# A graph attention layer with one head: the four row sums, the old sum and the clearing of rows change places

## The chip, the cores and the metric

The kernel runs on one core of a Trainium2 chip. The metric is the device time of one launch in microseconds (us); the times below are of the kernel before the change. The engines are TensorE (PE; its weight loads are listed as PEld), VectorE (DVE), ScalarE (ACT), GpSimd (POOL) and SyncE (SP, which here only issues DMAs).

## The reference, cut to what matters

A graph has 1250 nodes and 20,000 edges, with rows of 768 floats. Two attention layers run one after the other (8 heads, then 1 head), and a relational layer and a graph convolution follow.

```python
def gatv2(x, src, dst, Ws, bs, Wd, bd, attn):
    fs = (x @ Ws + bs).reshape(-1, H, D)
    fd = (x @ Wd + bd).reshape(-1, H, D)
    e = leaky_relu(fs[src] + fd[dst], 0.2)
    logits = einsum('ehd,hd->eh', e, attn)
    m = segment_max(logits, dst, num_segments=N)
    ex = exp(logits - m[dst])
    denom = segment_sum(ex, dst, num_segments=N)
    alpha = ex / denom[dst]
    out = segment_sum(alpha[:, :, None] * fs[src], dst, num_segments=N)
    return elu(out)
h = gatv2(x, ..., W1s, ..., attn1)        # 8 heads of 96
h = layer_norm(h + x, ln1_w, ln1_b)
out = gatv2(h, ..., Wos, ..., attno)      # 1 head of 768: the "second attention"
return layer_norm(out, lno_w, lno_b)
```

## The kernel before

**Tiles and groups.** The nodes are sorted by degree and laid out in 10 tiles of 128. A *group* is 128 nodes of one tile with S = 4 incoming edges each. There are 48 groups in this input, run as 12 turns of a loop with U = 4 groups in its body (index `u`). The softmax is kept running: each group brings four rows, its logits raise the maximum `top`, the sum so far in `acc` is scaled down by a factor, and the group's weighted rows are added.

**The stages.** Each stage ends at a barrier of all engines: sorting of edges, projection of x, the first attention (`attention("first", HEADS, ...)`), `settle(True)`, which normalises and projects for the second attention, the second attention (`attention("second", 1, ...)`), `settle(False)`, the 34 relations, two gather stages and the output. The change touches the second attention and `settle(True)`.

**A group in the second attention.** The order on each engine is the order of its code; semaphores join them.

- POOL (`gather_edges`) gathers the edge record (L799) and, two groups ahead, the four rows `row` of 128 x 776 (L804, four DMAs). Between them it makes the masks `val` and `neg` (L826 to L829). A row buffer is free again when PE has counted `summed` for the group that used it.
- The sum fs + fd: DVE adds `fdt` to rows 0 and 1 (L1049). PE adds it to rows 2 and 3 in PSUM (`pS`), as a product of the identity with the row and one with `fdt` (L994, L996).
- DVE takes the leaky part times the attention vector with its sum for all four rows (L1072), in PSUM for two of them. This gives the logits.
- DVE `arguments` (L1090 to L1100) makes the exponents. ACT takes the exponential (L970) and scales the old sum, `scaled` = `acc` times the factor (L977).
- DVE `weigh` (L1106 to L1121) makes four diagonal matrices `shares` from the weights (L1110, four instructions). PE multiplies them with the four rows into `pA` (L1014). DVE `finish` (L1079) adds `pA` and `scaled` into `acc`.

**The order within a turn.** DVE does, for each u: `arguments(u)`, `add(u + 1)` (the sums and logits of the next group), `finish(u - 1)`, `weigh(u)`. PE does `add(u + 2)` and then the four products of group u. Each product of PE with f32 operands of 128 x 384 appears in the trace as two passes, and a row has two halves, so a row's product is four passes.

**The clearing.** The relational stage writes only some of the rows of `y_d`; the others are set to zero before it. SP does this with a loop of DMAs from a zeroed tile `nothing` (L932), each waited for before the next one is issued. It runs in the second attention's SP block, beside the groups.

Of the kernel before, what the change touches and what calls it, by code (L numbers as in the profile page):

```python
# [11 lines left out]
P = 128  # L12
# [55 lines left out]
def gnn_kernel(nc, io, out):  # L68
    ctx = ExitStack()
    with ctx:  # L70
# [800 lines left out]
        def attention(name, heads, attn, fd_table):  # L871
# [5 lines left out]
            with stage() as st:  # L877
# [19 lines left out]
                pS = [pb(f"pS{j}", [P, 2, 512], F32, st) for j in range(S // 2)]  # L897
                nothing = sb("nothing", [P, D], F32, st)
                att_in, dve_step, init_ok, fd_in, zeroed, y_zero, sp_posted = sems(
                    st, "att_in", "dve_step", "init_ok", "fd_in", "zeroed", "y_zero", "sp_posted")  # L900
                sum_ok = Signal(st, "sum_ok", S // 2, U, U)
# [17 lines left out]
                with nc.Block() as block:  # L919
                    @block.sync  # L920
                    def _(sp):
                        sp.dma_start(attr[:], attn.rearrange("h d -> (h d)").partition_broadcast(P)).then_inc(att_in, 16)
                        sp.wait_ge(att_in, 16)
                        if fd_table is None:

                            sp.wait_ge(zeroed, 1)

                            tiles = tiles_of(sp)
                            behind = sp.value_load(ctl[0:1, C_BEHIND:C_BEHIND + 1], min_val=1, max_val=RT)
                            with sp.Fori(0, behind) as n:  # L930
                                sp.wait_ge(y_zero, n * 16)
                                sp.dma_start(y_d[ds(((tiles + n) * P).with_bounds(min_val=0, max_val=RT * P), P), :],  # L932
                                             nothing[:]).then_inc(y_zero, 16)
                            sp.wait_ge(y_zero, behind * 16)
                            sp.sem_inc(sp_posted, 1)

# [82 lines left out]
                    def _(dve):  # L1019
# [4 lines left out]
                        v = Steps(dve, dve_step)  # L1024
                        dve.memset(nothing[:], 0.0).then_inc(zeroed, 1)
                        v.mark(dve.memset(acc[:], 0.0))
# [110 lines left out]
                        finish(turns, -1, last)  # L1137

        attention("first", HEADS, io["L0_gnn_attn1"], fd_d[0:N])

        rcnt = sb("rcnt", [P, NT + 1, RELS], F32)

        def settle(first):
# [11 lines left out]
            with stage() as st:  # L1155
# [25 lines left out]
                placed = sems(st, "placed0", "placed1")  # L1181
                f_out = sems(st, "f_out0", "f_out1")
                low_ok = Signal(st, "low_ok", 1, 2, 2)
                exp_ok = Signal(st, "exp_ok", 1, 2, 2)
# [31 lines left out]
                with nc.Block() as block:  # L1216
                    @block.sync
                    def _(sp):
# [8 lines left out]
                        sp.wait_ge(v_in, 16 * (NW + 3))  # L1227
                        sp.wait_ge(w_in, 16 * NW)

                    @block.gpsimd  # L1230
# [115 lines left out]
                    def _(dve):  # L1346
# [6 lines left out]
                        pre.link(dve.reciprocal(rden[:], rden[:]))  # L1353
                        if first:
                            for b in range(2):
                                pre.link(dve.memset(of[b][:, D:W], 0.0))
                        else:
                            pre.link(dve.tensor_reduce(csum[:], cntge[:].rearrange("p t (s r) -> p t r s", s=S), X, ALU.add))
                            pre.link(dve.tensor_copy(csum[:, :, 0], degr[:]))
                            pre.link(dve.tensor_tensor(rcnt[:], csum[:, :, 0:RELS], csum[:, :, 1:RELS + 1], ALU.subtract))  # L1360
                            pre.link(dve.tensor_scalar(rcnt[:], rcnt[:], 1.0, None, ALU.max))
                            pre.link(dve.reciprocal(rcnt[:], rcnt[:]))
# [83 lines left out]

        settle(True)
        attention("second", 1, io["L0_gnn_attno"], None)
        settle(False)


# [423 lines left out]
```

## Time and profile before

| | |
|---|---|
| median of 3 runs | 4282.16 us (4281.59 to 4284.36) |
| the profiled execution's own time | 4274.83 us |
| its span | 4273.1 us |
| `settle(True)` | about 1132 to 1336 us of the span |
| second attention | about 1337 to 1885 us of the span |
| `settle(False)` | from about 1886 us |

The rows that the prediction uses come from this execution. *Granted clock* is the TensorE clock that the chip allowed, 1.00 for 2.4 GHz and 0.5 for 1.2 GHz. "Idle before" an instruction is put down to whatever released it last. "x2" in a timeline row is two passes merged, with the time from the start of the first to the end of the last.

### The profile page before, as it was taken

What the parts mean: (1) busy time and instruction counts of PE and PEld (TensorE: products, weight loads), DVE (VectorE), ACT (ScalarE), POOL (GpSimd) and SP (SyncE); (2) the same over time, 40 slices, a digit from 0 to 9 for tenths busy, and PEclk for the clock granted to TensorE, in tenths of its full rate; (3) what the DMA queues carried; (4) which work ended last, traced back from release to release, by engine and by line L of the source; (5) the groups of instructions that cost most, each with busy time, mean ns of one, the idle gap of its engine ahead of it and who ended that gap; (6) DMA issues with size and microseconds to landing.
All of it is one profiled execution on the core that took longest, in us unless ns stands there. A gap on an engine that the chain in (4) does not pass through costs nothing. (4 is left out here: it accounts for less than half of the span.)

```text
span 4273.1 us, 61931 instructions
## 1 busy us (share of the span) xinstructions
PE 2822.8 (66%) x12224; PEld 2123.7 (50%) x12225; DVE 2608.4 (61%) x5744; ACT 1177.6 (28%) x4467; POOL 2034.2 (48%) x2781
## 2 busy tenths in 40 slices
PE   0295877778697999967799999999997000080000
PEld 0153444444354555533599999999997000040000
DVE  8234888888666788866555555555553666515555
ACT  0011655566421111113344444444443000010000
POOL 0474766667456777731111111111112777517776
PEclk6697988998898999988899999999999555595555
DMA  0233433333314765541355556555554666506665
GB/s 23 87 90 116 120 105 105 105 105 106 133 41 136 249 202 151 152 133 45 113 184 181 185 175 185 183 180 182 177 182 141 183 187 183 181 37 203 196 203 176
DMA packets 198954, 621.95 MB, mean 146 GB/s; under 512 B 42375, under 2 KB 87259, under 8 KB 198683
## 3 DMA queue, kind: packets, MB, share of 16 engines
q0 software_dynamic: 95696, 414.22, 32.6%
q1 hardware_dynamic: 53628, 139.21, 10.6%
q10 hardware_dynamic: 49536, 67.66, 4.4%
q14 instruction: 83, 0.68, 0.0%
q8 instruction: 11, 0.18, 0.0%
HBM read 503.34 MB, written 117.91 MB: 145 GB/s over the span
## 5 line engine op out<-in xcount | busy, mean ns | idle before, releaser
L1603 PE MATMUL pO<-wh,gT 128*128 128x384 f32 x4128 | 1093.0, 338 | 0.5 <-DVE wl L1641 0.5
L1603 PEld LDWEIGHTS pO<-wh,gT 128*128 128x128 f32 x4128 | 749.8, 188 | 0.8 <-DVE wl L1641 0.8
L1603 PE MATMUL pO<-wl,gT 128*128 128x384 f32 x2064 | 691.1, 335 | 0.0
L804 POOL DMA_INDIRECT row<-fs_d,rec x400 | 441.1, 1103 | 163.0 <-issue 122.0
L994 PE MATMUL pS<-row,ident 128*128 128x384 f32 x800 | 361.6, 536 | 237.7 <-DVE sj L1069 149.5
L1627 DVE TENSOR_SCALAR cntge<-pT 128x768 int32<-128x768 int32 x173 | 165.6, 957 | 566.7 <-PE pT L501 563.7
L508 PE MATMUL pO<-wt,hT 128*128 128x384 f32 (+1 forms) x1200 | 420.1, 512 | 41.4 <-ACT hT L1314 19.6
L1556 ACT ACTIVATE gT<-cntge 128x256 fp32r<-128x256 f32 x1038 | 371.7, 411 | 165.0 <-PE pO L1603 122.9
L501 PE MATMUL pT<-ident,ht 128*128 128x128 f32 (+1 forms) x240 | 39.6, 310 | 558.0 <-ACT ht L1764 440.7
L960 ACT ACTIVATE sj<-sj 128x96 f32<-128x96 f32 x1176 | 313.0, 268 | 281.7 <-DVE sj L1069 281.7
L1603 PEld LDWEIGHTS pO<-wl,gT 128*128 128x128 f32 x2064 | 388.7, 188 | 0.0
L994 PEld LDWEIGHTS pS<-row,ident 128*128 128x128 f32 x800 | 159.3, 208 | 381.2 <-DVE sj L1069 183.9
L996 PE MATMUL pS<-fdt,ident 128*128 (+1 forms) x800 | 346.8, 517 | 0.0
L1538 POOL COPY gindex<-source 128x1 int32 x172 | 49.8, 289 | 621.3 <-DMA g<-hr_d,gindex 621.3
L508 PEld LDWEIGHTS pO<-wt,hT 128*128 128x128 f32 (+1 forms) x1200 | 236.7, 200 | 214.9 <-issue 68.5
L1527 POOL DMA_INDIRECT g<-hr_d,gindex x173 | 168.9, 976 | 355.4 <-PE pT L501 350.2
L501 PEld LDWEIGHTS pT<-ident,ht 128*128 128x128 f32 (+1 forms) x240 | 32.3, 159 | 574.2 <-ACT ht L1764 441.0
L1566 ACT ACTIVATE nrow<-pO 128x384 f32<-128x384 f32 x344 | 166.0, 483 | 537.2 <-PE pO L1603 537.2
L1719 DVE SCALAR_TENSOR_TENSOR acc<-row,val,acc 128x768 f32 x192 | 196.5, 1024 | 155.8 <-DMA row<-xs_d,rec 150.7
L799 POOL DMA_INDIRECT rec<-by_dst_d,index x204 | 219.3, 1075 | 85.3 <-issue 78.9
L804 POOL DMA_INDIRECT row<-xs_d,rec x200 | 226.3, 1131 | 61.9 <-issue 61.6
L1014 PE MATMUL pA<-row,shares 128*128 128x384 f32 x768 | 255.5, 486 | 0.0
(287 smaller groups left out, 5019.7 us busy)
## 6 DMA issues: line engine op xcount, KB each, us to landing
raw<-in_L_gnn_W_rel_dram SPq DMA_DIRECT2D x204, 384.0 KB
y_d<-nrow ACTq DMA_DIRECT2D x344, 192.0 KB
y_d<-nothing SPq DMA_DIRECT2D x53, 384.0 KB, 2.7
row<-fs_d,rec POOLq DMA_INDIRECT x400, 4.6
fs_d<-of SPq DMA_DIRECT2D x9, 388.0 KB
fd_d<-of SPq DMA_DIRECT2D x9, 388.0 KB, 2.6
xt<-in_x_dram SPq DMA_DIRECT2D x9, 384.0 KB, 4.2
h_d<-ht SPq DMA_DIRECT2D x9, 384.0 KB, 4.1
```

Of the source, the lines that this page charges most:

```text
L508: last = pe.matmul(dst[0:rows, q, 0:HALF], rows_t[:, c * P:c * P + rows], w[:, c, lo:up], start=c == 0, stop=c == KC - 1)
L799: pool.indirect_dma_start(b["rec"][u][:], None, table_rows, bass.IndirectOffsetOnAxis(ap=b["index"][u][:], axis=0)).then_inc(b["rec_in"][u ...
L804: pool.indirect_dma_start(b["row"][u][:, j, :], None, table, bass.IndirectOffsetOnAxis(ap=b["rec"][u][:, 2 * j + field:2 * j + field + 1], ...
L960: last = act.activation(of_head, of_head, ACT.Copy, accum_out=dots[off % U][:, j, h:h + 1])
L994: pe.matmul(pS[j][:, q, 0:HALF], ident[:], row[off % U][:, S // 2 + j, lo:up], start=True, stop=False)
L996: last = pe.matmul(pS[j][:, q, 0:HALF], ident[:], fdt_row(tile)[:, lo:up], start=False, stop=True)
L1014: last = pe.matmul(pA[:, q, 0:HALF], share, row[u][:, j, lo:up], start=j == 0, stop=j == S - 1)
L1527: pool.indirect_dma_start(g[:], None, hr_d, bass.IndirectOffsetOnAxis(ap=gindex[:], axis=0))\
L1556: act.activation(gT[:, c].bitcast(F32R), cut[:, :, c * P:(c + 1) * P], ACT.Copy).then_inc(gT_ok.sem, 1)
L1566: act.activation(y[:, lo:up], pO[:, q, 0:HALF], ACT.Copy).then_inc(evac_ok.sem, 1)
L1603: last = pe.matmul(pO[:, q, 0:HALF], gT[:, c, half, :].bitcast(F32R), w[:, c, lo:up].bitcast(F32R), start=c == 0 and k == 0, stop=c == KC ...
L1719: dve.scalar_tensor_tensor(out=into, in0=b["row"][u][:, j, :], scalar=w[:, j:j + 1], in1=into, op0=ALU.mult, op1=ALU.add).then_inc(used.se ...
```

## The change

A function `attention_single` takes the place of `attention` for one head.

- PE adds `fdt` to row 3 alone; DVE adds it to rows 0, 1 and 2. `pS` has two buffers, one for each of two groups.
- The diagonal matrices become one tile `share` of five, made by one instruction of 128 x 640. The fifth (index 0) holds the factor of the old sum. PE multiplies it with `acc` as a last product into `pA`. `pA` has two buffers.
- ACT no longer scales the old sum; it moves the finished `pA` into `acc`.
- `finish` on DVE is gone.
- The order on PE is now: the products of group u, then the old sum's product, then `add(u + 2)`. The order on DVE is `arguments(u)`, `dot(u + 1)`, `weigh(u)`.
- The clearing of `y_d` and its zeroed tile move into the SP and DVE blocks of `settle(True)`. There SP reaches it after its waits for the stage's weights.

The diff, cut to its core (the memset and the SP loop are removed from `attention` word for word as they stand in `settle` below):

```diff
+        def attention_single():
+            BY_PE = S - 1
...
+                    @block.scalar
+                    def _(act):
...
+                        def keep(i, off, tile):
+                            total.wait(act, i, off)
+                            act.activation(split(of(acc, tile)), halves(pA[off % 2]), ACT.Copy).then_inc(kept.sem, 1)
...
+                            for u in range(U):
+                                ex_in.wait(act, i, u)
+                                shared.wait(act, i, u - 2)
+                                act.activation(pe_[u % 2][:], ex[u % 2][:], ACT.Exp).then_inc(ex_ok.sem, 1)
+                                keep(i, u - 1, t[u])
...
+                        def add(i, off, tile):
+                            rows_wait(pe, b, i, off)
+                            logits.wait(pe, i, off - 2)
+                            for q, lo, up in HB:
+                                pe.matmul(pS[off % 2][:, q, 0:HALF], ident[:], row[off % U][:, BY_PE, lo:up],
+                                          start=True, stop=False)
+                                last = pe.matmul(pS[off % 2][:, q, 0:HALF], ident[:], of(fdt, tile)[:, lo:up],
+                                                 start=False, stop=True)
+                            last.then_inc(sum_pe.sem, 1)
...
+                            for u in range(U):
+                                shared.wait(pe, i, u)
+                                kept.wait(pe, i, u - 2)
+                                for j in range(S):
+                                    for q, lo, up in HB:
+                                        last = pe.matmul(pA[u % 2][:, q, 0:HALF], share[u % 2][:, 1 + j, :], row[u][:, j, lo:up],
+                                                         start=j == 0, stop=False)
+                                last.then_inc(summed.sem, 1)
+                                kept.wait(pe, i, u - 1)
+                                for q, lo, up in HB:
+                                    last = pe.matmul(pA[u % 2][:, q, 0:HALF], share[u % 2][:, 0, :], of(acc, t[u])[:, lo:up],
+                                                     start=False, stop=True)
+                                last.then_inc(total.sem, 1)
+                                add(i, u + 2, t[u + 2])
...
+                        def dot(i, off, tile):
+                            rows_wait(dve, b, i, off)
...
+                            for j in range(BY_PE):
+                                logits.wait(dve, i, off - 1, j + 1)
+                                dve.tensor_tensor(leak[:, j, :], row[off % U][:, j, 0:D], fd[:, 0:D], ALU.add)\
+                                   .then_inc(sum_ok.sem, 1)
...
+                            for j in range(S):
+                                if j < BY_PE:
+                                    sum_ok.wait(dve, i, off, j + 1)
+                                    ins = dict(out=leak[:, j, :], in0=leak[:, j, :], in1=attr[:])
+                                else:
+                                    logits.wait(dve, i, off - 1, j + 1)
+                                    sum_pe.wait(dve, i, off)
+                                    ins = dict(out=split(leak[:, j, :]), in0=halves(pS[off % 2]), in1=split(attr[:]))
...
+                        def weigh(v, i, u, tile):
+                            k = u % 2
+                            ex_ok.wait(dve, i, u)
+                            v.link(dve.tensor_tensor(pe_[k][:, 1:S + 1, 0], pe_[k][:, 1:S + 1, 0], val[u][:], ALU.mult))
+                            total.wait(dve, i, u - 2)
+                            den_ok.wait(dve, i, u - 1)
+                            sh = [P, S + 1, P]
+                            v.mark(dve.tensor_tensor(share[k][:], over(ident[:], 1, sh), pe_[k][:].to_broadcast(sh), ALU.mult))
+                            v.mark(dve.tensor_reduce(dsum[:], pe_[k][:, 1:S + 1, 0], X, ALU.add))
...
+                            v.wait()
+                            dve.sem_inc(shared.sem, 1)
...
+                            for u in range(U):
+                                top_ok.wait(dve, i, u - 1)
+                                arguments(v, i, u, t[u])
+                                dot(i, u + 1, t[u + 1])
+                                weigh(v, i, u, t[u])
...
+                        if first:
+                            sp.wait_ge(zeroed, 1)
+                            tiles = tiles_of(sp)
+                            behind = sp.value_load(ctl[0:1, C_BEHIND:C_BEHIND + 1], min_val=1, max_val=RT)
+                            with sp.Fori(0, behind) as n:
+                                sp.wait_ge(y_zero, n * 16)
+                                sp.dma_start(y_d[ds(((tiles + n) * P).with_bounds(min_val=0, max_val=RT * P), P), :],
+                                             nothing[:]).then_inc(y_zero, 16)
+                            sp.wait_ge(y_zero, behind * 16)
+                            sp.sem_inc(sp_posted, 1)
...
-        attention("second", 1, io["L0_gnn_attno"], None)
+        attention_single()
```

On PE, in the loop of the second attention, where one group's sums meet another group's products. Before (the last sums of group 3, then the products of group 1; `row1_2` is row buffer 1 of this stage, and REGISTER_ALU and ISA are address and semaphore work):

```order
L994 MATMUL pS1_2<-row3_2,ident 128x384
L996 MATMUL pS1_2<-fdt,ident 128x384
L994 MATMUL pS1_2<-row3_2,ident 128x384
L996 MATMUL pS1_2<-fdt,ident 128x384
L555 REGISTER_ALU x2
L1014 MATMUL pA_2<-row1_2,shares 128x384 x2
L555 REGISTER_ALU
L1014 MATMUL pA_2<-row1_2,shares 128x384 x6
```

And now, at the same place:

```order
L1221 MATMUL pA1<-row1_2,share1 128x384 x8
L1226 REGISTER_ALU x2
L1226 ISA
L1226 MATMUL pA1<-acc,share1 128x384
L1226 ISA
L1226 MATMUL pA1<-acc,share1 128x384
L555 REGISTER_ALU
L1204 MATMUL pS1_2<-row3_2,ident 128x384
L1206 REGISTER_ALU x2
L1206 ISA
L1206 MATMUL pS1_2<-fdt,ident 128x384
```

The sums of group u + 2 stood ahead of the products of group u and stand behind them now; the product with `acc` has come in between.

On DVE, the end of one group's logits and what follows, in the same loop. Before:

```order
L1072 SCALAR_TENSOR_TENSOR sj,dots_2<-pS_2,attr 128x768 x2
L555 REGISTER_ALU
L1079 REGISTER_ALU
L1079 ISA
L1079 TENSOR_TENSOR acc<-pA,scaled 128x768
L1106 TENSOR_TENSOR pe_2<-pe_2,val_2 128x4
L50 REGISTER_ALU
L1110 TENSOR_SCALAR shares<-ident,pe_2 128x128 x4
L1117 TENSOR_REDUCE dsum<-pe_2 128x1
```

And now:

```order
L1266 SCALAR_TENSOR_TENSOR leak,dots_2<-leak,attr 128x768
L555 REGISTER_ALU
L1266 SCALAR_TENSOR_TENSOR leak,dots_2<-pS_2,attr 128x768
L1289 TENSOR_TENSOR pe_2<-pe_2,val_2 128x4
L50 REGISTER_ALU
L1293 TENSOR_TENSOR share<-ident,pe_2 128x640
L1294 TENSOR_REDUCE dsum<-pe_2 128x1
```

The step on `pA` is gone, one of the two steps that read `pS` is left and is the last one ahead of the weights, and four diagonal instructions have become one.

## Rows read from the trace of the kernel before

**Rows 1.** Busy time by stretch: us, PE, PEld, DVE, ACT, POOL, granted clock, DMA share, GB/s.

```profile
1217.00:1237.00 20.00, 18.94 (x64) 11.23 (x63) 13.84 (x23) 5.98 (x7) 13.78 (x14) 1.00 0.16 40
...
1375.00:1560.00 185.00, 180.81 (x554) 103.88 (x553) 147.84 (x460) 24.56 (x38) 132.51 (x188) 1.00 0.72 244
1560.00:1885.00 325.00, 319.50 (x980) 184.47 (x978) 259.45 (x804) 43.08 (x66) 221.96 (x321) 1.00 0.49 146
```

**Rows 2.** Second attention's PE passes with `shares`: durations in ns, first and last start.

```profile
L1014 PE MATMUL pA<-row,shares x768: 486/486/486, 1378.6 to 1882.9; 128*128 128x384 f32 x192
```

**Rows 3.** Groups of instructions by shape, 1560 to 1870 us: busy us, mean ns, idle before.

```profile
L1049 DVE TENSOR_TENSOR sj<-row,fdt 128x768 f32<-128x768 f32 x60 | 54.8, 954 | 10.3 <-issue 10.3
...
L977 ACT ACTIVATE scaled<-acc,pe 128x768 f32 x29 | 27.1, 936 | 223.5 <-DVE acc L1079 223.5
```

**Rows 4.** Timeline of one group of the second attention: start, us, engine, instruction.

```profile
1604.31 5.32 PE L1014 MATMUL pA<-row,shares 128*128 128x384 f32 x16
...
1607.07 0.95 DVE L1072 SCALAR_TENSOR_TENSOR sj<-pS,attr 128x768 f32<-128x768 f32 x1
...
1607.95 0.08 DVE L1072 DVE_READ_ACCUMULATOR sj<-pS,attr 128x1 f32 x1
...
1610.46 0.95 POOL L804 DMA_INDIRECT row<-fs_d,rec  x1 [0.99 <-PE pA L1014]
1610.65 0.15 DVE L1106 TENSOR_TENSOR pe<-pe,val 128x4 f32<-128x4 f32 x1
...
1610.84 0.88 DVE L1110 TENSOR_SCALAR shares<-ident,pe 128x128 f32<-128x128 f32 x4
...
1611.64 0.14 DVE L1117 TENSOR_REDUCE dsum<-pe 128x1 f32<-128x4 f32 x1
...
1611.88 0.16 DVE L1121 TENSOR_TENSOR den<-den,dsum 128x1 f32 x1
...
1621.15 0.95 POOL L804 DMA_INDIRECT row<-fs_d,rec  x1 [0.30 <-issue]
```

**Rows 5.** Timeline of the stage's first groups: where DVE waits for a sum of PE.

```profile
1358.21 0.81 PE L996 MATMUL pS<-fdt,ident 128*128 128x384 f32 x2
...
1359.06 0.96 DVE L1072 SCALAR_TENSOR_TENSOR sj<-pS,attr 128x768 f32<-128x768 f32 x1 [0.90 <-PE pS L996]
...
1371.09 0.95 DVE L1079 TENSOR_TENSOR acc<-pA,scaled 128x768 f32 x1
```

**Rows 6.** Timeline of the first attention: PE's first passes after it sat idle.

```profile
463.84 0.91 PE L994 MATMUL pS<-row,ident 128*128 128x384 f32 x2 [1.84 <-DMA row<-fs_d,rec]
...
508.65 1.65 PE L994 MATMUL pS<-row,ident 128*128 128x384 f32 x2 [2.76 <-DVE sj L1069]
...
941.65 1.65 PE L994 MATMUL pS<-row,ident 128*128 128x384 f32 x2 [2.42 <-DVE sj L1069]
...
1120.03 0.91 PE L994 MATMUL pS<-row,ident 128*128 128x384 f32 x2 [2.41 <-DVE sj L1069]
```

**Rows 7.** Busy time by stretch, columns as in Rows 1: behind two of these pauses.

```profile
508.00:515.00 7.00, 6.35 (x10) 3.52 (x11) 6.79 (x13) 7.00 (x52) 4.93 (x7) 0.51 0.26 65
...
941.00:947.00 6.00, 5.35 (x12) 3.08 (x13) 5.97 (x9) 6.00 (x47) 4.26 (x7) 0.72 0.00 0
```

**Rows 8.** The clearing by its tile: SP's issues in ns, first and last start.

```profile
L932 SPq DMA_DIRECT2D y_d<-nothing x53: 332/332/370, 1342.8 to 1543.4; - x53
...
L932 SPq DMA_DIRECT2D y_d<-nothing x2: 332/332/332, 1522.2 to 1524.6; - x2
```

**Rows 9.** DMA issues by line: KB each, us to landing.

```profile
wt<-in_L_gnn_Wod_dram SPq DMA_DIRECT2D x1, 2304.0 KB, 20.3
```

**Rows 10.** Timeline: SP's last load of `settle(True)`, DVE's last copy, the next stage's memset.

```profile
1136.46 0.69 SPq L1226 DMA_DIRECT2D wt<-in_L_gnn_Wod_dram  x1
...
1336.11 0.14 DVE L1442 COPY fdt<-lin 128x1 f32<-128x1 f32 x1
...
1338.74 0.70 DVE L1025 MEMSET nothing<- 128x768 f32 x1 [2.48 <-issue]
```

More of the change, by code:

```diff
@@ L897, in attention @@
                 pS = [pb(f"pS{j}", [P, 2, 512], F32, st) for j in range(S // 2)]
-                nothing = sb("nothing", [P, D], F32, st)
-                att_in, dve_step, init_ok, fd_in, zeroed, y_zero, sp_posted = sems(
-                    st, "att_in", "dve_step", "init_ok", "fd_in", "zeroed", "y_zero", "sp_posted")
+                att_in, dve_step, init_ok, fd_in = sems(st, "att_in", "dve_step", "init_ok", "fd_in")
                 sum_ok = Signal(st, "sum_ok", S // 2, U, U)
@@ L923, in _ @@
                         sp.wait_ge(att_in, 16)
[L924 to L935, printed above, removed]
                     @block.gpsimd
@@ L1024, in _ @@
                         v = Steps(dve, dve_step)
-                        dve.memset(nothing[:], 0.0).then_inc(zeroed, 1)
                         v.mark(dve.memset(acc[:], 0.0))
@@ L1182, in settle @@
                 f_out = sems(st, "f_out0", "f_out1")
+                if first:
+                    nothing = sb("nothing", [P, D], F32, st)
+                    zeroed, y_zero, sp_posted = sems(st, "zeroed", "y_zero", "sp_posted")
                 low_ok = Signal(st, "low_ok", 1, 2, 2)
@@ L1228, in _ @@
                         sp.wait_ge(w_in, 16 * NW)
+                        if first:
+                            sp.wait_ge(zeroed, 1)
[7 more added lines that the diff above has]
+                            sp.sem_inc(sp_posted, 1)
                     @block.gpsimd
@@ L1354, in _ @@
                         if first:
+                            dve.memset(nothing[:], 0.0).then_inc(zeroed, 1)
                             for b in range(2):
```

108 lines of the change are left out of this document (added).

## The prediction

> **What bounds the kernel now.** The views were read in this order: the busy time by stretch, the passes of one tile, the groups of instructions, and then the timeline of single groups. The first shows that in the second attention PE is busy in 319.5 of 325 us, at the full clock of 2.4 GHz, while DVE is busy in 259.5 [rows 1]. So PE's passes set the pace there. The pace: the first of the 768 passes with `shares` starts at 1378.6 and the last at 1882.9, and that last one is the 16th of its group [rows 2]. Sixteen passes last 5.32 us and a single one 0.486, so they start (5.32 - 0.486) / 15 = 0.322 apart [rows 2, 4]. A group's period is then (1882.9 - 15 x 0.322 - 1378.6) / 47 = 10.63 us. PE's own need is 32 passes (16 for two row sums, 16 for four products) x 0.322 = 10.3. PE never waits long, because the sums of group u + 2 stand ahead of the products of group u: while PE does them, DVE makes the weights that the products need. The reader should note that this order, more than the number of passes, is what keeps PE busy.
>
> **PE's passes: fewer.** One row sum is dropped (8 passes), and the old sum's product is added (4). 28 passes x 0.322 = 9.0 us of work. If nothing else changed, PE would allow 1.3 us less per group.
>
> **DVE's work: about the same.** It gains one sum of 954 ns [rows 3] and loses the step on `pA`, 0.95 [rows 5]. Four diagonal instructions, 0.88 together [rows 4], become one of 640 elements. No row has that form. It is sized between 0.15 for 4 elements and 954 ns for 768 [rows 3, 4]: (0.954 - 0.15) / 764 = 1.05 ns an element, so 0.15 + 636 x 0.00105 = 0.82 us, and the next instruction starts some 0.08 before its end, as it does behind the four: 0.74. The ends: 0.6 if it ran faster than a two-operand step, 0.9 if it ran as slowly as the four. DVE's busy time stays 259.45 / 325 x 10.63 = 8.5 us per group, and with its short waits between small steps about 9.3.
>
> **ACT.** The move of `pA` replaces the scaling, 936 ns [rows 3]. Reading PSUM may make it shorter, or at worst twice as long. ACT sits idle for 223.5 us in 29 groups, 7.7 each [rows 3], and PE asks for the moved sum only behind 16 passes of the next group, so I cost it at nothing. If that cover were gone, its 0.9 would be paid in full.
>
> **The order: this is the main term.** Now PE does the products of group u - 1, the old sum, and only then `add(u + 1)`. DVE reads that sum in the last step of `dot(u + 1)`, which stands ahead of `weigh(u)`, and PE can't start group u without the weights. So the two wait for each other in turn, and a period is the sum of four pieces:
> - DVE from the read of `pS` to the signal `shared`: 0.88 for the step (1607.07 to 1607.95), 0.19 for the weights' mask (1610.65 to 1610.84), 0.74 for `share`, 0.24 for the two small steps (1611.64 to 1611.88) [rows 4]. Sum 2.05.
> - The signal to PE. No row isolates it; PE's signal to DVE took 0.04, from 1358.21 + 0.81 to 1359.06 [rows 5]. I take 0.05; the ends are 0.02 and 0.3.
> - PE: 27 x 0.322 + 0.486 = 9.18, and 0.10 more, since two passes behind a pause take 0.91 and not 0.81 [rows 5, 6]. Sum 9.28.
> - The signal back, 0.04 [rows 5].
>
> The period is 2.05 + 0.05 + 9.28 + 0.04 = 11.42 us, against 10.63. That is 0.79 x 47 = 37 us **more**. DVE's remaining work, 9.3 - 2.05 = 7.3, and the few register loads at a turn's start fit beside PE's 9.28. The ends of the stage change little: the first group no longer waits behind a step on `pA`, which started at 1371.09 [rows 5], and the last group has the old sum, the move and a superfluous `add` behind it. I take 0, with 3 us either way.
>
> **PE's clock.** PE now pauses 11.42 - 9.28 = 2.1 us in each group. In the first attention PE also pauses, and what follows is in the rows: behind 1.84 us its first two passes take 0.91, behind 2.76 us they take 1.65; behind 2.42 us they take 1.65, and behind 2.41 us 0.91 [rows 6]. The two long ones go with a granted clock of 0.51 over 7 us and 0.72 over 6 us [rows 7], so PE was at 1.2 GHz for nearly all of the first stretch and for 0.56 of the second. The second costs 6 x 0.28 = 1.7 us, the first 7 x 0.49 = 3.4. A pause of 2.1 lies between one that cost nothing and a pair of which one cost. I take one group in four at 1.7, the nearer row: 0.43 x 47 = 20 us. The ends are 0 and one fall in each group, 80 us. All of it would lie on the path, since PE is in the chain.
>
> **The clearing.** In `settle(True)` SP can begin when the last weights have landed, 1136.46 + 20.3 = 1156.8 [rows 9, 10], and its register loads are done; these took from the end of the memset, 1339.44 [rows 10], to 1342.8 [rows 8], 3.4 us. So it begins at 1160.2. Its 53 DMAs ran one behind the other at (1543.4 - 1342.8) / 52 = 3.86 us, and at 2.4 where nothing was in the way [rows 8]. The stage's last work ends at 1336.11 + 0.14 = 1336.25 [rows 10], so there are 176 us, or 3.3 us for each. The DMA engines' share is 0.16 in `settle(True)` and 0.49 in the attention when the clearing is over [rows 1]; by that, a third of the 1.46 us between the two paces: 53 x 2.9 = 154, done by 1314. Hidden: nothing is paid, and nothing is gained in the attention, where PE was as busy with the clearing beside it (180.8 of 185) as without [rows 1]. If the old pace held, the last would land at 1160.2 + 53 x 3.86 = 1364.8, and the barrier would come 28 us late. The moved memset, 0.70 [rows 10], stands ahead of the stage's first step: +0.7.
>
> A rule speaks against this cover. The Trainium skill, "DMA: Bandwidth & Descriptors", section "Issuing engines are not separate DMA queues", says that DMAs issued by SP and by GpSimd end up on the same 16 DMA engines and interleave. By that rule moving the clearing to another stage doesn't take its competition away, and with as many transfers of GpSimd beside it as before the sum would be 28 us higher; the trace's long and short times between issues agree that it is slowed by others.
>
> **The sum.** 37 + 20 + 0.7 = 58 us. The profiled execution took 4274.8 us, 7.3 below the median of the three runs, so it would become 4332; against the median, 4282.2 + 58 = **4340 us**.
>
> **Rivals.**
> - *The clock falls in most groups.* Each fall costs 1.7 at least and so makes the period longer without making the pause shorter; nothing in the loop cures it. With a fall in most groups, 47 x (0.79 + 1.4) = 103, so 4386. For it: one of the two pauses of 2.4 fell. Against: the pause here is shorter than those. 28%.
> - *The clearing outlasts its stage*, at the old pace: 4340 + 28 = 4368. For it: SP waits for each DMA. Against: the share of 0.16. 6%.
> - *The other side: the loop isn't closed through the new order.* The decisive point is whether PE's sum for the next group is there when DVE comes to read it. If DVE found it ready, because the four pieces come to less than 10.6 together (0.8 less than my sum), then the pace would be that of POOL, whose own turn from gather to gather is 1621.15 - 1610.46 = 10.69 with its slow masks and, by the wait of 0.30 to 0.99 ahead of it, hardly under 10.3 [rows 4]. A period of 10.3 gives 47 x (-0.33) = -15, so 4267. For it: PE has 4 passes less and buffers are doubled. Against: the order of the rows on both engines has no way round. 7%.
> - *The serial loop as computed, few falls:* 4340, itself between 4310 (short `share`, no fall) and 4365. 59%.
>
> **How the numbers follow.** About 0.2% (8.6 us) is what a measurement of this kernel can tell from no change. The range reaches from 4308, the serial loop with its cheap ends, to 4400, a fall in nearly every group with the serial loop's upper ends; it leaves out the faster case, part of the clearing's sum with the clock's, and the very worst. Of the 7% on the other side I give 5 to faster and 2 to same, and 1 more to same for a serial loop with all its pieces at their low ends. Faster 0.05, same 0.03, slower 0.92.
>
> **What would show it.** In the trace of the changed kernel: the passes with `share` at a period of 11.4 to 12.5 us; the step of DVE on `pS` waiting for PE some 1.5 to 2 us in each group; PE waiting about 2.1 us for the DVE ahead of the first product with `share`; a granted clock of 0.9 to 1.0 in the stage, and under 0.9 if the second case holds; POOL waiting for PE by about 1 us per group, where it hardly did. The last `y_d` DMA should be issued by 1315, with `settle(True)` ending at 1337. The prediction is wrong if DVE doesn't wait at `pS`, if the period is under 10.6, or if SP is the last at the barrier of `settle(True)`.

## The result, and the profile after

| | before | after |
|---|---|---|
| median on the same chip (4 runs each) | 4281.88 us (4277.8 to 4284.36) | 4378.73 us (4373.06 to 4383.2) |
| ratio, 95% interval | | 1.0226 (1.0209 to 1.0244) |
| profiled execution's own time / span | 4274.83 / 4273.1 us | 4381.81 / 4380.1 us |
| second attention | 547.9 us | 643.5 us |

The change costs 97 us. The forecast was 58 us and its range 26 to 118. The stage's time runs between two rows of SP, its first DMA in the stage and its first in `settle(False)`. Timeline of before:

```profile
1337.67 0.34 SPq L922 DMA_DIRECT2D attr<-in_L_gnn_attno_dram  x1
...
1885.58 0.34 SPq L1219 DMA_DIRECT2D lnw<-in_L_gnn_lno_w_dram  x1
```

And of after:

```profile
1341.16 0.34 SPq L1165 DMA_DIRECT2D attr<-in_L_gnn_attno_dram  x1
...
1984.65 0.34 SPq L1396 DMA_DIRECT2D lnw<-in_L_gnn_lno_w_dram  x1
```

So the stage has nearly all of it: 643.5 - 547.9 = 95.6 us, with 1.2 more in `settle(True)` by the same kind of rows. (The two profiled executions are 107 us apart. The other 10 lie in stages ahead and behind whose code is the same, and the four executions of the changed kernel alone spread over 10 us.) The passes with `share` and DVE's instruction that makes it (after, by tile: durations in ns, first and last start):

```profile
L1221 PE MATMUL pA<-row,share x768: 486/486/1004, 1373.9 to 1979.4; 128*128 128x384 f32 x192
...
L1293 DVE TENSOR_TENSOR share<-ident,pe x48: 824/826/846, 1372.8 to 1973.4; 128x640 f32<-128x640 f32 x48
```

The period is (1973.4 - 1372.8) / 47 = **12.78 us**, where [rows 2] gave 10.63. Some passes last up to 1004 ns. The busy time by stretch (after, columns as in Rows 1) says the same of the whole stage: PE is busy in 83% of the time, where [rows 1] show 98%, and the granted clock is 0.90.

```profile
1400.00:1560.00 160.00, 132.53 (x354) 73.35 (x355) 111.81 (x308) 16.29 (x28) 86.08 (x142) 0.90 0.41 129
1560.00:1700.00 140.00, 115.73 (x310) 63.73 (x309) 95.42 (x265) 15.06 (x25) 72.62 (x121) 0.90 0.41 125
1700.00:1960.00 260.00, 214.98 (x572) 118.35 (x570) 174.76 (x483) 27.61 (x46) 139.81 (x224) 0.90 0.41 125
```

The loop itself is in the timeline (after; start, us, engine, instruction):

```profile
1449.96 0.96 DVE L1266 SCALAR_TENSOR_TENSOR leak<-pS,attr 128x768 f32<-128x768 f32 x1 [3.46 <-PE pS L1206]
...
1451.03 0.83 DVE L1293 TENSOR_TENSOR share<-ident,pe 128x640 f32<-128x640 f32 x1
...
1452.10 5.43 PE L1221 MATMUL pA<-row,share 128*128 128x384 f32 x16 [2.18 <-DVEq L1298]
...
1460.59 0.81 PE L1206 MATMUL pS<-fdt,ident 128*128 x2
1461.44 0.96 DVE L1266 SCALAR_TENSOR_TENSOR leak<-pS,attr 128x768 f32<-128x768 f32 x1 [1.79 <-PE pS L1206]
...
1463.59 7.12 PE L1221 MATMUL pA<-row,share 128*128 128x384 f32 x16 [2.18 <-DVEq L1298]
```

Read it down: DVE takes the sum in `pS` at 1449.96, makes `share`, and PE starts at 1452.10; PE's last sum ends at 1461.40, and DVE, which has stood for 1.79 us, takes it at 1461.44. Each engine waits for the other once in a group. One turn is 2.14 + 9.30 + 0.04 = 11.48. The next group begins behind a pause of the same 2.18 us, but its sixteen passes last 7.12 us instead of 5.43, and the group took 13.25. Not all of the sixteen are slow: by stretches of 1 us from 1464 to 1468 the granted clock was 0.59, 0.50, 0.50 and 0.70, and it was 1.00 ahead of them and behind, so about 3.4 us ran at 1.2 GHz.

Groups of instructions (after, 1400 to 1960 us; busy us, mean ns, idle before):

```profile
L1221 PE MATMUL pA<-row,share 128*128 128x384 f32 x704 | 292.9, 580 | 97.1 <-DVEq L1298 97.1
...
L1266 DVE SCALAR_TENSOR_TENSOR leak<-pS,attr 128x768 f32<-128x768 f32 x44 | 42.1, 958 | 118.4 <-PE pS L1206 118.4
...
L804 POOL DMA_INDIRECT row<-fs_d,rec x179 | 174.4, 974 | 190.5 <-PE pA L1221 147.5 <-issue 43.0
...
L1181 ACT ACTIVATE acc<-pA 128x768 f32 x44 | 35.7, 811 | 250.3 <-PE pA L1226 250.3
```

POOL now waits 147.5 / 44 = 3.4 us per group; it isn't what holds the stage up. The clearing, by its tile (after):

```profile
L1412 SPq DMA_DIRECT2D y_d<-nothing x53: 332/333/376, 1161.0 to 1303.0; - x53
```

### The profile page after: what moved, and what is told of

Same layout as the page of the kernel before. It is cut to its first block and busy times, and to the rows that moved or that the text cites. A ratio compares the mean times of both kernels' runs of the same rounds, so it can differ in the third digit from the quotient of the medians.

```text
span 4380.1 us, 61353 instructions
## 1 busy us (share of the span) xinstructions
PE 2822.5 (64%) x12016; PEld 2111.0 (48%) x12017; DVE 2610.7 (60%) x5599; ACT 1158.8 (26%) x4468; POOL 1980.6 (45%) x2781
## 5 line engine op out<-in xcount | busy, mean ns | idle before, releaser
L804 POOL DMA_INDIRECT row<-fs_d,rec x400 | 424.8, 1062 | 302.1 <-PE pA L1221 147.5
L1744 ACT ACTIVATE gT<-cntge 128x256 fp32r<-128x256 f32 x1038 | 358.0, 408 | 182.3 <-PE pO L1791 139.1
L1221 PE MATMUL pA<-row,share 128*128 128x384 f32 x768 | 320.5, 581 | 113.0 <-DVEq L1298 113.0
L980 PE MATMUL pS<-row,ident 128*128 128x384 f32 x400 | 192.5, 567 | 209.9 <-DVE sj L1054 161.5
L1221 PEld LDWEIGHTS pA<-row,share 128*128 128x128 f32 x768 | 169.6, 226 | 263.8 <-DVEq L1298 100.9
L799 POOL DMA_INDIRECT rec<-by_dst_d,index x204 | 237.6, 1164 | 86.6 <-issue 83.7
L1000 PE MATMUL pA<-row,ident 128*128 128x384 f32 x768 | 255.5, 486 | 0.0
```

The costliest lines, as they stand in the source:

```text
L799: pool.indirect_dma_start(b["rec"][u][:], None, table_rows, bass.IndirectOffsetOnAxis(ap=b["index"][u][:], axis=0)).then_inc(b["rec_in"][u ...
L804: pool.indirect_dma_start(b["row"][u][:, j, :], None, table, bass.IndirectOffsetOnAxis(ap=b["rec"][u][:, 2 * j + field:2 * j + field + 1], ...
L980: pe.matmul(pS[j][:, q, 0:HALF], ident[:], row[off % U][:, S // 2 + j, lo:up], start=True, stop=False)
L1000: last = pe.matmul(pA[:, q, 0:HALF], share, row[u][:, j, lo:up], start=j == 0, stop=j == S - 1)
L1221: last = pe.matmul(pA[u % 2][:, q, 0:HALF], share[u % 2][:, 1 + j, :], row[u][:, j, lo:up], start=j == 0, stop=False)
L1744: act.activation(gT[:, c].bitcast(F32R), cut[:, :, c * P:(c + 1) * P], ACT.Copy).then_inc(gT_ok.sem, 1)
```

## The experiments

The theory after the result: the order closes the loop (some 40 us), and the clock falls behind most of the pauses that the loop makes (some 60). The rival: one of the other parts costs the time (the product with `acc`, the third sum on DVE, the moved clearing, POOL). Each ratio below is to the kernel before on the same chip, with its 95% interval.

### The order alone, undone and done

In the changed kernel, PE's sums go back ahead of the products:

```diff
                             for u in range(U):
+                                add(i, u + 2, t[u + 2])
                                 shared.wait(pe, i, u)
...
-                                add(i, u + 2, t[u + 2])
```

> The changed kernel with one thing moved back: PE does the sums of group u + 2 ahead of the products of group u, as before the change. Theory (PE and DVE wait for each other in turn because the sums stand behind the products): the wait of DVE at pS, 1.8 to 3.5 us a group, goes, and so does PE's pause of 2.2; the period drops from 12.78 to the next bound, POOL's own turn of 10.3 to 10.7 us, so 4270 to 4290 us. Rival 1 (the new work itself is what costs: the product with the old sum, its move by ACT, one more sum on DVE): the period stays near 12.8, about 4379 us. Rival 2 (only the clock's falls cost): 11.5 a group, about 4318 us.

Measured: 4284.61 us, 1.0005 (0.9995 to 1.0015). One line takes back the whole loss. The kernel with the sums first, by tile and by stretch:

```profile
L1293 DVE TENSOR_TENSOR share<-ident,pe x48: 824/826/828, 1373.0 to 1873.6; 128x640 f32<-128x640 f32 x48
```

```profile
1560.00:1700.00 140.00, 121.23 (x367) 68.38 (x366) 112.28 (x315) 16.42 (x29) 102.75 (x144) 1.00 0.52 148
```

The period is 500.6 / 47 = 10.65, the clock full. But PE has 4 passes fewer than before and still gains nothing. Its groups (1400 to 1840 us) show that it waits for rows, and that POOL, which fetches them, waits for nobody ("issue" is POOL's own time between its instructions):

```profile
L804 POOL DMA_INDIRECT row<-fs_d,rec x166 | 214.4, 1291 | 50.9 <-issue 50.9
...
L1204 PE MATMUL pS<-row,ident 128*128 128x384 f32 x164 | 70.4, 511 | 56.8 <-DMA row<-fs_d,rec 56.8
```

The same edit the other way round, in the kernel before: PE's sums behind the products, nothing else changed.

```diff
                             for u in range(U):
-                                add(i, u + 2, t[u])
...
+                                if heads == 1:
+                                    add(i, u + 2, t[u])
```

> The kernel before the change with only PE's order in the second attention taken from the change: products of group u first, the sums of group u + 2 behind them. No other part of the change. Theory: the loop closes here too; 0.88 (last step on pS) + 0.87 (step on pA) + 0.19 + 0.28 (first diagonal matrix) + 0.05 + 10.57 (32 passes) + 0.04 = 12.9 us at full clock with a pause of 2.3, and 1.7 more where the clock falls: 4282 + 47 x (12.9 - 10.63) = 4389 us without falls, up to 4469 with one in every group, 4450 with three in four. Rival (the order alone does little as long as PE has 32 passes to keep it busy): 4282 to 4300 us.

Measured: 4425.59 us, 1.0334 (1.0317 to 1.0351). Its groups (1400 to 1840 us):

```profile
L1014 PE MATMUL pA<-row,shares 128*128 128x384 f32 x514 | 197.4, 543 | 74.4 <-DVE shares L1112 72.0 <-DVE acc L1081 2.3
...
L1074 DVE SCALAR_TENSOR_TENSOR sj<-pS,attr 128x768 f32<-128x768 f32 x65 | 62.3, 958 | 119.7 <-PE pS L996 107.0 <-issue 12.7
```

The same mutual waits, without any other part of the change. With two rows in `pS` to read and 32 passes the loop is longer, and it costs 142 us. The timeline of PE divides them: a group without a slow clock takes 12.91 us (from 1408.02 to 1420.93), as the expectation had it, which makes (12.91 - 10.63) x 47 = 107, and 21 of the 47 groups behind a pause of 2.32 us or a little more are slower, by 1.5 to 1.7 us each. The order is the cause in both kernels.

A third way to open the loop leaves PE's order as changed and moves DVE's step on `pS` behind `weigh`:

```diff
-                            for j in range(S):
+                            logits_of(i, off, range(BY_PE))
...
                                 weigh(v, i, u, t[u])
+                                logits_of(i, u + 1, [BY_PE])
```

> The changed kernel with PE's order as changed, but DVE takes the last step of the next group's logits, the one that reads pS, behind weigh instead of ahead of it. Theory (a loop through both engines): opening it on DVE's side is as good as on PE's side, period 10.3 to 10.7 us, 4270 to 4295 us, and PE is ahead of DVE at pS. Rival (it is the place of PE's sums that costs, whatever DVE's order, since rows and PSUM come free later): near 4379 us.

Measured: 4291.86 us, 1.0025 (1.0013 to 1.0036). The loop is open; the period is 10.98, and POOL again waits for nobody.

### The clock alone

Three products of PE (six passes) whose result isn't used are put into the pause, behind the sums; then one product only:

```diff
                                 add(i, u + 2, t[u + 2])
+                                for k in range(3):
+                                    pe.matmul(pA[(u + 1) % 2][:, k % 2, 0:HALF], ident[:], fdt[:, 0, 0:HALF],
+                                              start=True, stop=True)
```

> The changed kernel with three further products behind the sums of each group (six passes, 1.9 us, identity by fdt into the pA buffer that the next group's first product overwrites), so that PE's pause of 2.2 us is shortened to about 0.3. The output is unchanged by it. Theory (three pauses in four are followed by passes at 1.2 GHz, 1.7 us each time): the granted clock is 1.00 through the stage, every period is 11.5 us, (12.78 - 11.49) x 47 = 61 us less than the changed kernel, 4318 us, though PE does more. Rival (the long periods of 13.2 us have another cause, such as the gathers): 4379 us, or up to 4379 + 1.9 x 48 = 4470 us if the six passes lie on the path.

> The changed kernel with one extra product of PE (two passes) in each group behind its sums, into a buffer that nobody reads then; so PE's pause for the DVE becomes about 1.55 us, where it was 2.2, and with three extra products about 0.3. Nothing else is changed. Theory (a pause of 1.55 costs nothing, as in the first attention one of 1.84 did not): the granted clock is 1.00, the period 11.5, and the time 4318 to 4327, as with three extra products. Rival (what matters is PE's work over the whole period and not the length of the pause): falls stay in most groups, 4360 to 4380.

Measured: 4326.67 us with three, 1.0101 (1.0085 to 1.0118), and 4324.52 with one, 1.0086 (1.0066 to 1.0106). **More work on the engine of the loop makes the kernel 52 and 54 us faster.** With one extra product, by stretch:

```profile
1560.00:1700.00 140.00, 119.86 (x362) 67.41 (x360) 106.92 (x294) 16.08 (x27) 105.25 (x134) 1.00 0.47 137
```

by tile:

```profile
L1296 DVE TENSOR_TENSOR share<-ident,pe x48: 824/826/827, 1374.6 to 1917.6; 128x640 f32<-128x640 f32 x48
```

and by groups (1400 to 1840 us):

```profile
L1221 PE MATMUL pA<-row,share 128*128 128x384 f32 x614 | 208.4, 493 | 60.8 <-DVEq L1301 59.3 <-issue 1.5
```

The clock is full again in all groups but the first, which starts behind a wait of 8.9 us. The period is 11.55, and PE still pauses 60.8 / 38 = 1.6 us in each group. So the loop as such is worth 1.0086 to 1.0101, 37 to 43 us, and the clock 1.0226 less these, 54 to 60 us. By periods the clock is (12.78 - 11.55) x 47 = 58, and by the timeline of the changed kernel 34 slow groups at 1.69 are 57.

### What a longer DVE costs, with the loop closed and open

The instruction that makes `share` is issued twice, the first into a spare tile that isn't used; once with the loop closed and the pause filled, once with the sums first.

```diff
+                            v.mark(dve.tensor_tensor(spare[:], over(ident[:], 1, sh), pe_[k][:].to_broadcast(sh), ALU.mult))
                             v.mark(dve.tensor_tensor(share[k][:], over(ident[:], 1, sh), pe_[k][:].to_broadcast(sh), ALU.mult))
```

> The changed kernel with the three further products on PE (as in fill, 4327 us) and the instruction that makes the five diagonal matrices issued twice, the first time into a tile that nobody reads. That adds 0.74 us to DVE's piece between reading pS and the signal to PE. Theory (closed loop, all pieces in a row): 47 x 0.74 = 35 us more than fill, 4362 us, and more if the longer pause lets the clock fall. Rival (DVE has room beside PE): as fill, 4327 us.

> The same doubled instruction in sums_first (4285 us), where PE's sums stand ahead. Theory (loop open; DVE needs about 9.4 us of its own and then 10.1, under POOL's turn of 10.65): no change, 4280 to 4292 us. Rival (DVE's work counts there too): 35 us more, 4320 us.

Measured: closed 4358.73 us, 1.0167 (1.0149 to 1.0185), which is 32 over the filled kernel: the loop passes on each DVE step between `pS` and the signal (the period went from 11.55 to 12.28, by 0.73). Open: 4309.99 us, 1.0064 (1.0047 to 1.0081), 25 more than with the step once, where none was expected. This is a miss. DVE stood 1.05 us per group for POOL's masks (43.3 / 41) in the kernel with the sums first and should have had room. The groups (1400 to 1840 us) show POOL still waiting for nobody, but its issues have become longer:

```profile
L804 POOL DMA_INDIRECT row<-fs_d,rec x157 | 216.6, 1380 | 48.8 <-issue 48.8
```

4 x (1.380 - 1.291) = 0.36 us for the rows and 0.23 for the four mask instructions make 0.59 a turn; the period is (1899.1 - 1370.5) / 47 = 11.25, which is 0.60 more. (The granted clock was 0.96 there, but PE stood 63.1 us for rows in 39 groups, so its falls lie in time that it had left.) A timeline of the kernel with the sums first shows how an issue becomes long:

```profile
1700.36 0.95 DVE L1266 SCALAR_TENSOR_TENSOR leak<-leak,attr 128x768 f32<-128x768 f32 x1
1700.62 1.51 POOL L804 DMA_INDIRECT row<-fs_d,rec  x1 [0.30 <-issue]
...
1702.12 0.95 DVE L1266 SCALAR_TENSOR_TENSOR leak<-pS,attr 128x768 f32<-128x768 f32 x1
1702.43 0.94 POOL L804 DMA_INDIRECT row<-fs_d,rec  x1 [0.30 <-issue]
1703.19 0.82 DVE L1293 TENSOR_TENSOR share<-ident,pe 128x640 f32<-128x640 f32 x1
1703.39 0.69 POOL L826 TENSOR_TENSOR over<-left,slot 128x4 f32<-128x4 f32 x1
```

Here an issue beside DVE steps with both large operands in SBUF takes 1.51 us, and one beside the step that reads `pS` in PSUM 0.94. The small mask takes 0.69 beside `share`, and 0.20 is the mean of the next one. To test it, the extra instruction was made a reduction over the same 640 elements, with one operand in SBUF and the same length:

```diff
+                            v.mark(dve.tensor_reduce(spare[:], over(ident[:], 1, sh), X, ALU.add))
```

> As the run with the sums first and the share instruction doubled, but the extra instruction is a tensor_reduce over the same 640 elements: it reads one operand in SBUF instead of two. Its result isn't used. Theory (POOL's turn is the pace, and its instructions become longer while DVE reads two operands in SBUF): the time goes back to 4284 to 4290, and POOL's gather instructions of rows to a mean of about 1.29 us, from 1.375. Rival (DVE's added time itself is on the path): about 4310 again, since the added instruction is about as long.

Measured: 4294.57 us, 1.0012 (1.0002 to 1.0022). By groups (1400 to 1840 us):

```profile
L804 POOL DMA_INDIRECT row<-fs_d,rec x164 | 209.0, 1274 | 50.9 <-issue 50.9
...
L1294 DVE TENSOR_REDUCE spare<-ident 128x5 f32<-128x640 f32 x40 | 32.9, 822 | 1.4
```

The same 0.82 us on DVE costs 3 us by the ratios, which is within their error, where the other cost 25. By the periods it is 0.17 x 47 = 8, where the other was 28. The issues are short again. So it isn't DVE's time that counts with the loop open, but what it does to POOL. The time is a few us above what was expected; the masks are 0.20 us longer in sum than with the sums first, nearly as much as beside the two-operand instruction (0.23). What the second operand makes of it thus shows in the issues, 0.36 against none, and not in the masks. The two instructions differ in their results too, 640 elements against 5; but the step that reads `pS` writes 768 and leaves an issue at 0.94.

The Trainium skill says it too: the page "GPSIMD Engine Reference", section "Specifications", has GpSimd's SBUF interfaces shared with VectorE, with contention when a VectorE instruction has two SBUF inputs. The rows of the issues agree; those of the masks don't tell one operand from two, and the page gives no size.

### The clearing alone

In the kernel before, only the clearing and its memset are moved, as in the change (the same lines).

```diff
-                        if fd_table is None:
-                            sp.wait_ge(zeroed, 1)
...
+                        if first:
+                            sp.wait_ge(zeroed, 1)
```

> The kernel before the change with only the clearing of y_d (its memset and SP's loop) moved into settle(True). Theory (hidden at both places): within 3 us of the kernel before; settle(True) about 1 us longer for the memset and the DMAs beside it, the second attention 0 to 3 us shorter. Rival (part of the change's 97 us is the clearing's): 10 us or more above the kernel before.

Measured: 4280.63 us, 0.9988 (0.9979 to 0.9997). By its tile:

```profile
L1223 SPq DMA_DIRECT2D y_d<-nothing x53: 332/332/381, 1164.4 to 1304.7; - x53
```

It is hidden, 2.7 us apart, and if anything a few us are gained: the attention took 544.1 us there and 547.9 in the profile of before.

### POOL's masks on ACT

The four mask instructions of POOL are made by five of ACT, a group ahead: in the changed kernel with the sums first, in the kernel before, and in the changed kernel as it is.

```diff
+                            m.link(act.activation(b["over"][:], b["slot"][:], ACT.Relu, bias=left, scale=-1.0))
+                            m.link(act.activation(inv[:], b["over"][:], ACT.Relu, bias=ones[:, 0:1], scale=-1.0))
+                            m.mark(act.activation(val[off % U][:], inv[:], ACT.Identity, bias=ones[:, 0:1], scale=-1.0))
+                            m.mark(act.activation(neg[off % U][:], inv[:], ACT.Copy, scale=-BIG))
+                            m.mark(act.activation(left, left, ACT.Identity, bias=minus[:]))
```

> sums_first with the masks of each group (val, neg and the count of edges left, four instructions of POOL) made by ACT one group ahead, in five instructions; POOL is left with the gathers and the record's index. Theory (in sums_first POOL's turn of 10.65 us is the bound, and PE's 28 passes and DVE's work would allow less): POOL's turn drops by about 1.9 us, the period becomes 9.3 to 9.9 us, the larger of PE's 9.0 and DVE's 9.3 and some waiting, so 4285 - 47 x (10.65 - 9.6) = 4236 us, range 4220 to 4255. Rival (the gathers' transfers themselves set 10.6, not POOL's instructions): 4285 us. A third way: the wait for ACT's masks or its move of pA delays DVE and PE, 4290 us or more.

> The kernel before, with the four mask instructions of POOL in the second attention made by ACT instead, as five instructions, one group ahead; nothing else is changed. Theory (in the kernel before PE's 32 passes set the pace, 32 x 0.322 = 10.3 us, and POOL's turn adds only the few tenths that the period of 10.63 has above this): about 4270, with a period of 10.3 to 10.4 and PE still at the full clock; so most of what the same step gained behind the changed work (a period of 9.96) is open to it only with PE's 28 passes. Rival (POOL's turn was the pace of both kernels): the same 9.9 to 10.0 and about 4250.

> The changed kernel in its own order, with the four mask instructions of POOL in the second attention made by ACT instead, as five instructions, one group ahead. Theory (the loop of DVE and PE sets the pace and POOL is no part of it): 4379, within 10, period about 12.8, POOL waiting for PE longer by what the masks took. Rival (the contention of POOL and DVE makes the loop's pieces on DVE longer, or POOL's turn is in the loop after all): below 4350.

Measured with the sums first: **4245.24 us, 0.9907 (0.9892 to 0.9923)**, faster than both kernels. By its tile the period is 9.96:

```profile
L1315 DVE TENSOR_TENSOR share<-ident,pe x48: 824/826/827, 1372.3 to 1840.4; 128x640 f32<-128x640 f32 x48
```

So POOL's turn was the pace once the order was right. That PE's four passes fewer are needed for this gain too isn't shown: the run on the kernel before, below, was to tell and doesn't.

In the changed order: 4385.12 us, 1.0230 (1.0210 to 1.0250), as the theory said. The loop has no POOL in it; relieving POOL there gives nothing.

In the kernel before: 4299.12 us, 1.0027 (1.0017 to 1.0038), where 4270 was expected. This is a miss, and it doesn't answer the question, since the edit brought a wait of its own. Timeline:

```profile
1700.01 0.94 ACT L998 ACTIVATE scaled<-acc,pe 128x768 f32 x1 [8.06 <-DVE acc L1106]
...
1702.22 0.16 DVE L1117 TENSOR_TENSOR lg<-dots,neg 128x4 f32<-128x4 f32 x1 [1.05 <-ACTq L966]
```

In the old kernel ACT must first scale the old sum, behind `finish`. The masks are queued behind it, and DVE waits for them. What POOL alone was worth before isn't settled. It may well have been near the pace there too: from 1400 to 1840 us of the kernel before, POOL waited for PE only 2.8 us ahead of its 165 row issues, and PE waited 5.0 us for rows. The table sums up:

| kernel | us | period | ratio |
|---|---|---|---|
| after | 4378.7 | 12.78 | 1.0226 |
| after, one extra product in the pause | 4324.5 | 11.55 | 1.0086 |
| after, sums first | 4284.6 | 10.65 | 1.0005 |
| the same, masks on ACT | 4245.2 | 9.96 | 0.9907 |

## Why the prediction was right or wrong

**The loop: right.** The four pieces were given as 2.05 + 0.05 + 9.28 + 0.04 = 11.42. The timeline has 2.14 (DVE and the signal), 9.30 and 0.04, and a group without a slow clock takes 11.48 to 11.56. That is (11.49 - 10.63) x 47 = 40 us, where 37 were forecast. Within it `share` was sized right, 0.82 for 0.826 measured.

**The clock: the mechanism right, the size wrong by a factor of three.** The step that failed is "I take one group in four at 1.7, the nearer row". What one fall costs was right: 7.12 - 5.43 = 1.69. How often was not. Of the 47 groups that start behind a pause of 2.18 to 2.27 us, 13 have sixteen passes in 5.43, and 34 have slow ones: nearly three in four. That is 57 us instead of 20. (The stage's first group is slow as well, behind a wait of 9.38 us; with it the sum by periods is (12.78 - 11.49) x 47 = 61.) The error lay in how four rows of the first attention were used. They were two pauses that cost nothing and two that did, and the value taken was below the share that they show themselves, on the ground that 2.1 us is shorter than 2.4. The four rows were a fair sample of that stage: the trace of the kernel before has 16 pauses of PE between 1.84 and 3.08 us there, the granted clock of the next 3 us was 0.50 to 0.71 behind eight and 1.00 behind the other eight, and the two longest cost nothing:

```profile
762.13 0.91 PE L994 MATMUL pS<-row,ident 128*128 128x384 f32 x2 [3.08 <-DVE sj L1069]
```

Above 2.4 us the length didn't sort them, and between 1.84 and 2.41 that stage has no pause, so nothing in the rows showed that 2.1 is safer. With their half, the sum would have been 47 x 0.5 x 1.7 = 40 us and the forecast 4360, nearer and still low. Why three in four fell here and one in two there stays open. The case that came about is the rival "the clock falls in most groups": 4386 forecast, 4379 measured, and it stood at 28%. Its terms, 0.79 and 1.4 us a group, were measured as 0.86 and 1.29 (the latter with the first group).

**The ends of the stage: taken as 0, they gave back 5.5 us.** The loop's 47 periods cost (12.78 - 10.63) x 47 = 101 us, and the stage as a whole grew by 95.6. PE's first product with `share` came 1373.9 - 1341.16 = 32.7 us into the stage, where it had been 1378.6 - 1337.67 = 40.9. In the new order it no longer stands behind the sums of the third group, whose rows arrive late; with the sums first again it came 37.5 into the stage, behind a wait of 8.5 us for those rows. The end of the stage took some 3 us more.

**The clearing: right.** It began at 1161.0 (forecast 1160.2), its last DMA was issued at 1303.0 (by 1314), and moving it alone costs nothing. The DMAs came 2.73 us apart, where 2.9 were taken and 3.86 was the upper bound. The rule of the Trainium skill that was weighed there (page "DMA: Bandwidth & Descriptors", section "Issuing engines are not separate DMA queues") has the DMAs of SP and GpSimd interleave on the same engines. The 2.73 agree with it, being above the 2.4 seen with nothing in the way; they cost the kernel nothing in this stage.

**ACT at nothing: right.** The move takes 811 ns, less than the 936 of the scaling, and ACT idles 250.3 us in 44 groups before it.

**What was to be seen.** PE's pause of about 2.1 us: 97.1 / 44 = 2.2. DVE at `pS`, 1.5 to 2 us: 1.79 in a group at full clock, 3.46 in a slow one, 2.7 on average. POOL's wait, about 1 us: 3.4. Part of that are the slow groups, and part is that POOL's own instructions became shorter (rows 974 ns a piece, from 1061 before; the four masks 0.93 us together, from 2.05). That this is because DVE stands still more often beside them is likely, and not tested.

**The rival on the other side** (POOL's turn as the pace) was rightly ruled out for this order, and with the order undone it is what came. Only its figure was wrong: "hardly under 10.3" was 10.65, and 4267 was 4285. Its turn isn't a fixed one. With the sums first its row issues take 1.29 us, from 1.06 before, which is 0.93 more for four, and its four masks 1.28 together, from 2.05, so that the two nearly cancel. DVE has three more steps with two SBUF operands there (a third sum, its product and `share`), and it no longer has the step on `pA` and the four diagonal ones; which of them does what wasn't taken apart.

## What to carry to other kernels

Before fewer passes of an engine are counted as a gain, follow the new order of both engines' queues once round: where a sum that the next step needs has moved behind work that needs this step, the two engines take turns, and the period is the sum of both. A pause of PE that comes back in each group of a loop can cost its clock on top of its own length: 1.69 us behind 34 of 47 pauses of 2.2 us here, nothing behind those of 1.5 to 1.6. Where rows show both outcomes behind like pauses, don't lower their share on a ground that the rows don't show. When a resource is freed and nothing is gained, look for the engine that waits for nobody, and for what lengthens its instructions.

## What the runs showed of the hardware

**Which pauses cost the clock.** In the kernel with DVE's late step (timeline of PE), pauses of different length stand side by side:

```profile
1569.46 5.43 PE L1221 MATMUL pA<-row,share 128*128 128x384 f32 x16 [1.94 <-DVEq L1301]
...
1591.37 5.42 PE L1221 MATMUL pA<-row,share 128*128 128x384 f32 x16 [1.61 <-DVEq L1301]
1602.83 7.12 PE L1221 MATMUL pA<-row,share 128*128 128x384 f32 x16 [2.17 <-DVEq L1301]
...
1636.21 7.12 PE L1221 MATMUL pA<-row,share 128*128 128x384 f32 x16 [1.91 <-DVEq L1301]
```

Of the 12 pauses of 1.87 to 2.17 us in this kernel's loop six cost the clock, and of the shorter ones none. None of the 1.54 to 1.62 us in the kernel with one extra product was followed by a fall. In the changed kernel all 47 pauses are 2.18 to 2.27, and still 13 are without one, one after each two or three that fell. In the kernel before with its sums last they are longer, 2.32 to 2.35 in a group of 12.91 us, and fewer cost the clock, 21 of 47. The length of the pause alone doesn't decide, then; what else does isn't settled by these runs. In the changed kernel each fall cost the same 1.69 us.

**POOL's issues beside DVE.** In the kernel with the sums first (timelines of POOL and DVE, 1400 to 1840 us), the 40 issues of a gather of rows that had less than 0.3 us of a DVE step with two large SBUF operands beside them took 0.94 to 0.95 us. Of the 127 others three took up to 1.0, 27 up to 1.4 and the rest more, mostly 1.43 to 1.57. Such a step isn't enough to make an issue long, though: in the changed kernel 43 of 54 issues beside one took no more than 1.0. What the issue must meet isn't settled. In a kernel whose pace is POOL's turn, an instruction of DVE that is itself off the path cost 0.60 us a turn in this way, and one of the same length with one operand 0.17.
